# A deformable convolution layer laid out by group and block of rows, with its shift weights built on GpSimd instead of spread by TensorE

## What is computed

```python
G, KS, OM = 8, 3, 32; K = 9; Cg = C // G          # 8 groups of 16 channels, 9 taps
val = xf @ w_value + b_value
om = (xf @ w_off + b_off).reshape(N, P, G, OM)
offset = om[..., :2 * K].reshape(N, P, G, K, 2); mask = om[..., 2 * K:3 * K]
sy = base_y + offset[..., 1]; sx = base_x + offset[..., 0]   # pixel + tap + offset
y0, x0 = floor(sy), floor(sx); ty, tx = sy - y0, sx - x0
for dy, dx, wgt in ((0,0,(1-ty)*(1-tx)), (0,1,(1-ty)*tx), (1,0,ty*(1-tx)), (1,1,ty*tx)):
    acc = acc + gather(y0 + dy, x0 + dx) * (wgt * valid)[..., None]
out = (acc * mask[..., None]).sum(axis=3).reshape(N, P, C) @ w_out + b_out
out = out * inv + (bn_beta - bn_mean * inv)
return out * sigmoid(out)
```

## Time and profile before

| | us |
|---|---|
| runs of the kernel before | 7273.37, 7284.04, 7289.94 |
| the profiled execution's own time | 7276.4 |
| its span (first to last instruction) | 7274.6 |
| TensorE busy, share of span | 5761.8, 79% |
| VectorE busy | 5787.2, 80% |
| ScalarE busy | 5315.5, 73% |
| GpSimd busy | 1442.7, 20% |
| stage of the deformable layer, in the span | 0 to 1160.7 |
| granted clock of TensorE, mean of the span | 0.918 |

### The profile page before, as it was taken

How to read it: one execution, slowest core, us unless ns; L and a number is a source line. 1 busy time by engine, 2 the same in 40 slices (tenths; PEclk the granted TensorE clock), 3 DMA queues, 4 the chain that set the end, 5 groups by cost and what they waited for, 6 DMA issues and landing times. The chain is left out here.

```text
span 7274.6 us, 89393 instructions
## 1 busy us (share of the span) xinstructions
PE 5761.8 (79%) x32962; PEld 2035.3 (28%) x32962; DVE 5787.2 (80%) x12358; ACT 5315.5 (73%) x3820; POOL 1442.7 (20%) x1695
## 2 busy tenths in 40 slices
PE   7888886788769998977777777887777787778787
PEld 3222222344324443422111222222222222222223
DVE  7888887676557765888777788989889898889996
ACT  3332322465545543589999999999999999999996
POOL 3444451000136654610000000000000000000002
PEclk8888887888879998989999999999999999999998
DMA  3111100101000000000000000000000000000000
GB/s 123 50 50 41 53 19 11 30 23 25 12 9 1 1 1 4 1 7 1 1 1 1 1 1 1 1 1 1 12 1 1 1 1 12 1 1 1 1 1 24
DMA packets 45167, 95.26 MB, mean 13 GB/s; under 512 B 7863, under 2 KB 9657, under 8 KB 43578
## 3 DMA queue, kind: packets, MB, share of 16 engines
q1 hardware_dynamic: 43834, 88.44, 3.7%
q0 software_dynamic: 896, 1.06, 0.1%
HBM read 39.14 MB, written 33.55 MB: 10 GB/s over the span
## 5 line engine op out<-in xcount | busy, mean ns | idle before, releaser
L2815 ACT ACTIVATE aa_tanh<-aa_tanh 128x4096 f32<-128x4096 f32 (+5 forms) x1120 | 3671.6, 3368 | 23.6 <-DVE aa_tanh L2995 23.3
L2995 DVE TENSOR_SCALAR aa_tanh<-aa_f_times,aa_g_bias 128x1024 f32<-128x1024 f32 (+18 forms) x5120 | 2986.3, 646 | 475.0 <-PE aa_scores L2861 468.4
L2861 PE MATMUL aa_scores<-aa_tanh,aa_w_spread 128*32 128x512 f32 (+8 forms) x18432 | 2168.4, 584 | 805.7 <-ACT aa_tanh L2815 801.3
L2861 PEld LDWEIGHTS aa_scores<-aa_tanh,aa_w_spread 128*32 128x32 f32 x18432 | 581.0, 112 | 2233.3 <-ACT aa_tanh L2815 1119.8
L2875 PE MATMUL aa_out_sum<-aa_weights,aa_normed 128*128 128x512 f32 (+3 forms) x1152 | 642.8, 642 | 59.6 <-DVE aa_weights L3004 56.9
L2783 POOL TENSOR_SCALAR aa_group_normed<-x_rows,norm_scale,aa_shift_plus 128x128 f32<-128x128 f32 x96 | 92.5, 975 | 2412.4 <-PE aa_turned L2902 1767.3
L860 PE MATMUL near_weights_spread<-near_tap_weights,near_spread_consts 36*64 36x512 f32 x3200 | 429.5, 648 | 66.1 <-DVE near_weighted L507 53.3
L2086 PE MATMUL qa_out<-qa_hidden_rows,qa_weights_in 128*128 128x512 f32 x1024 | 475.3, 607 | 0.0
L880 PE MATMUL near_out_sum<-near_weighted,near_w_out 128*128 128x512 f32 x576 | 359.1, 756 | 103.5 <-DVE near_weighted L507 103.5
L496 DVE TENSOR_TENSOR near_weights_spread<-near_weights_spread,near_values 128x1024 f32<-128x1024 f32 x256 | 314.0, 1227 | 124.1 <-PE near_weights_spread L860 123.6
L427 POOL TENSOR_TENSOR near_tap_weights<-near_hat_y_mask,near_hat_x 128x1024 f32<-128x1024 f32 x144 | 340.0, 2372 | 279.0 <-PE near_weights_spread L860 220.1
(11 more groups left out here) (433 smaller groups left out, 6772.3 us busy)
## 6 DMA issues: line engine op xcount, KB each, us to landing
near_offsets<-near_offset_staged SPq DMA_DIRECT2D x45, 512.0 KB, 3.0
l_taps<-l_scan_in_out SPq DMA_DIRECT2D x256, 64.0 KB, 2.0
x_rows<-in_x SPq DMA_DIRECT2D x4, 2048.0 KB, 15.1
near_offset_y<-near_offsets SPq DMA_DIRECT2D x15, 512.0 KB, 4.0
near_offset_x<-near_offsets SPq DMA_DIRECT2D x15, 512.0 KB, 4.5
near_mask<-near_offsets SPq DMA_DIRECT2D x15, 512.0 KB, 5.4
out_x<-x_rows SPq DMA_DIRECT2D x3, 2048.0 KB, 6.3
out_x<-x_rows SPq DMA_DIRECT2D x8, 256.0 KB, 2.0
```

Source lines behind the costliest of these rows:

```text
L2815: a.activation(TH[:, u % PLACES, 0:length], TH[:, u % PLACES, 0:length], ACT.Tanh).then_inc(th_ready, 1)
L2861: last = t.matmul(sp_[32 * q:32 * q + 32, n % 2, s:e], W2S[:, tt, :], TH[:, p, o + s:o + e], start=tt == 0, stop=tt == 3, tile_position=(0 ...
L2995: ins = v.tensor_scalar(TH[:, p, at[q]:at[q] + w - s], FR[:, m % 2, lo + s:CHUNK], GB[:, key:key + 1], None, ALU.add)
```

## The change

The layout of the work changes. A partition is now (group, block of 4 rows): 8 groups x 16 blocks. A unit is row u of each block, and the free dimension of a product is 16 channels x 64 pixels. Weights of a shift then have 64 elements a partition, and VectorE reads them for each of the 16 channels with step zero. So:

- GpSimd builds the 25 weights of a unit itself: 9 products of hats (128x576, nine taps x 64 pixels), and 9 sums that add each to a 3 x 3 window of the 5 x 5 weights. The spreading matmuls, their constants and the rotating PSUM buffers go.
- Values go to DRAM (`values_at`) and are read back by SP into the new layout, row by row of the blocks, in a ring of 10 rows; offsets and masks are read back 9 rows x 16 blocks at a time, 8 DMAs for each kind. The runs are 64 elements.
- `product` reads both operands from SBUF and writes `PR` or a PSUM buffer `tmp`; `add` comes one shift later. Groups have 2, 1, 2, 1, ... shifts: 16 groups, 9 sums a unit, four buffers `PR`.
- TensorE adds the groups with the identity (`group_out`); ScalarE copies the sum (`keep_sums`, item "e"), SP writes it to DRAM (`sums_at`) and reads it back with channels on partitions (`read_sums`); `out_rows` (item "y") then multiplies by `w_out` and adds the correction for far taps.
- One PSUM buffer `wp` serves all prepared items. `FM` now lies in the buffer of the output `YB`, so that `keep_offsets` waits for `add_out`.
- Batches 1 to 3 of `x` are loaded by ScalarE's DMA queue. The steps for far taps come at other shifts.

The core of the diff:

```diff
-        SIZES = [3] * 7 + [2, 2]
+        SIZES = [2, 1] * 7 + [2, 2]
+            if U and t == 2:
+                items.append(("e", U - 1))
+            if U and t == 12:
+                items.append(("y", U - 1))
+            v = (22, 24) if U == 0 else (6, 8)
+            if u < 2 and b + 1 < NB and t in v:
+                items.append(("v", b + 1, 2 * u + v.index(t)))
+            if t in (16, 18, 20) and U + 4 < NU:
+                items.append(("o", U + 4, KINDS[(t - 16) // 2]))
...
+                        sp.dma_start(O[D_BLK * g:D_BLK * (g + 1), kind, :, :], parked[b][kind, 64 * h + K * gg:64 * h + K * (gg + 1), u, :].rearrange("k (y w) -> y k w", w=WW)).then_inc((ox_loaded, oy_loaded, mk_loaded)[kind], 16)
...
+                    for g in range(G):
+                        rows = values_at[b][D_CG * g:D_CG * (g + 1), j * WW:(j + D_BLK * D_BR) * WW].rearrange("c (y r w) -> y c r w", y=D_BLK, w=WW)[:, :, 0, :]
+                        sp.dma_start(V[D_BLK * g:D_BLK * (g + 1), :, ring_row(b, j) * D_ROWW + D_SPAN:(ring_row(b, j) + 1) * D_ROWW], rows).then_inc(v_loaded, 16)
...
+            def build_step(U, a, b):
...
+                pool.wait_ge(hym, 1 + U * D_NA + a + 1)
+                pool.wait_ge(hx_ready, 1 + U * D_NA + b + 1)
...
+                pool.tensor_tensor(q, HY[:, a, :, :], HX[:, b, :, :], ALU.mult).then_inc(tapped, 1)
+                pool.wait_ge(tapped, 1 + n + 1)
...
+                w = W[:, U % 2, a:a + 3, b:b + 3, :]
+                pool.tensor_tensor(w, w, q.rearrange("p (i j) w -> p i j w", i=3), ALU.add).then_inc(w_ready, 1)
...
+            for U in range(-1, NU):
+                nxt = U + 1
+                if nxt < NU:
+                    clear_weights(nxt)
+                for a in range(D_NA):
+                    if nxt < NU:
+                        mask_hat(nxt, a)
+                    for b in range(D_NA):
+                        if nxt < NU:
+                            build_step(nxt, a, b)
+                        if U > 0 and U % 4 == 0 and (a, b) == (1, 1):
+                            gather_offsets(U // 4)
+                        if U > 0 and U % 4 == 0 and (a, b) == (2, 0):
+                            gather_corners(U // 4)
+                        if U > 0 and (a, b) == (2, 0):
+                            add_out(U - 1)
+                if U == 0:
+                    gather_offsets(0)
+                    gather_corners(0)
...
+                if t == 0:
+                    v.wait_ge(w_ready, 1 + 10 * (U + 1))
...
+                v.tensor_tensor(out.rearrange("p (c w) -> p c w", w=WW), W[:, U % 2, dy + D_SPAN, dx + D_SPAN, :].unsqueeze(1).to_broadcast([P, D_CG, WW]),
+                                V[:, :, at:at + WW], ALU.mult).then_inc(prod, 1)
...
+            CHAIN = {(0, 10): rank_far, (0, 13): select_far, (0, 17): locate, (0, 21): corners, (0, 24): gather_sum, (1, 5): event_values}
+            CHAIN_AGAIN = {(-1, 23): rank_far, (0, 2): select_far, (0, 8): locate, (0, 12): corners, (0, 17): gather_sum, (0, 24): event_values}
...
+                    if t == 22 and U + 4 < NU:
+                        find_far(U + 4)
...
+                if kind == 1:
+                    if U:
                         a.wait_ge(ev_done, 1 + U)
+                    if U >= 5:
+                        a.wait_ge(x_done, 1 + U - 4)
...
+            def hats(U):
+                a.wait_ge(oy_loaded, 1 + 8 * 16 * (U + 1))
+                a.wait_ge(ox_loaded, 1 + 8 * 16 * (U + 1))
+                if U:
+                    a.wait_ge(w_ready, 1 + 10 * U)
...
+                    if t == (10 if U == 0 else 3) and U + 1 < NU:
+                        hats(U + 1)
...
+            def out_rows(U):
...
+                t.wait_ge(sums_in, 1 + 16 * G * (U + 1))
...
+                for s in range(2):
+                    t.matmul(wp[:, s, :], WO[:, :], OUT[:, s * BANK:(s + 1) * BANK], start=True, stop=False)
+                    last = t.matmul(wp[:, s, :], CORR[:, b % 2, :], OH[:, s, :], start=False, stop=True)
...
+                    last = t.matmul(acc[:, s, :], C["ident"], PR[:, gi % NSUM, s * BANK:(s + 1) * BANK], start=g == 0, stop=g == NGR - 1)
```

More of the change, by code:

```diff
@@ L287, in deform_near @@
-        order = list(prep)
+            if U and t == 2:
[7 more added lines that the diff above has]
+                items.append(("o", U + 4, KINDS[(t - 16) // 2]))
+            if U == 0 and t in (12, 15):
+                items.append(("c", 0, (12, 15).index(t)))
@@ L288, in deform_near @@
+            if U == 1 and t in (1, 3, 7):
+                items.append(("c", 0, 2 + (1, 3, 7).index(t)))
+            if b and u == 0 and t in (1, 6, 20, 22):
+                items.append(("c", b, (1, 6, 20, 22).index(t)))
+            if b and u == 1 and t == 3:
+                items.append(("c", b, 4))
+            return items
+        prep = [("b", 0), ("o", 0, 1), ("o", 0, 0), ("o", 0, 2)] + [("v", 0, i) for i in range(4)]
+        first_prep = list(prep)
         for U in range(NU):
             for t in range(NSH):
-                order += [("s", U, t)] + prepared(U, t)
@@ L291, in deform_near @@
                 prep += prepared(U, t)
-        PAIR = {z: i for i, z in enumerate(order)}
-        USE = {z: i for i, z in enumerate(prep)}
-        def spills_done(eng, U, kind):
-            if U == 0:
-                eng.wait_ge(spilled_first, 1 + 3 * 16)
-            else:
-                k = staged(U, kind)
-                eng.wait_ge(spilled[k % 2], 1 + 16 * (k // 2 + 1))
+        for U, kind in ((NU - 1, "e"), (NU - 1, "y")):
+            prep.append((kind, U))
+        in_ring = [z for z in prep if z[0] != "e"]
@@ new lines, in _ @@
+            for z in first_prep:
+                if z[0] in "ov":
+                    spill_item(z)
+                if z == ("o", 0, 2):
+                    for kind in KINDS:
+                        load_offsets(0, kind)
+            sp.wait_ge(padded, 1 + 2 * NB * 16)
+            load_values(0, 0, 8)
+            for U in range(NU):
+                b, u = divmod(U, 4)
+                here = [z for t in range(NSH) for z in prepared(U, t)]
+                if b and u == 0:
+                    load_values(b, 5, 8)
+                if u == 3 and b + 1 < NB:
+                    load_values(b + 1, 4, 5)
+                for z in here:
+                    if z[0] == "e" or (z[0] == "o" and z[1] < 4):
+                        spill_item(z)
+                    if z[0] == "e":
+                        read_sums(z[1])
+                    if z == ("o", 1, 2):
+                        for kind in KINDS:
+                            load_offsets(1, kind)
+                if U:
+                    for z in here:
+                        if z[0] == "v":
+                            spill_item(z)
+                if U + 2 < NU:
+                    load_offsets(U + 2, 1)
+                    load_offsets(U + 2, 0)
+                if u == 2 and b + 1 < NB:
+                    load_values(b + 1, 0, 4)
+                for z in here:
+                    if z[0] == "o" and z[1] >= 4:
+                        spill_item(z)
+                if U == 0:
+                    for z in here:
+                        if z[0] == "v":
+                            spill_item(z)
+                if U + 2 < NU:
+                    load_offsets(U + 2, 2)
```

696 lines of the change are left out of this document (308 added, 388 removed).

## The result

| | before | after |
|---|---|---|
| median of the runs, us | 7278.74 (4 runs, 7273.37 to 7289.94) | 7370.89 (4 runs, 7366.43 to 7373.73) |
| ratio, 95% interval | | 1.0124 (1.0106 to 1.0142) |
| span of the profiled execution, us | 7274.6 | 7368.8 |
| end of the deformable layer in the span | 1160.7 | 1249.7 |
| behind the layer | 6113.9 | 6119.1 |

What follows compares the result with a forecast made beforehand. VectorE bounds the kernel before, TensorE close behind; afterwards VectorE waits for GpSimd. Start 210, units 1 to 14 991, unit 15 40, end 26: 1267 against 1160.7, +106 us, so 7390, range 7265 to 7500.

Steps and rivals of the forecast that it cites:

- The exclusion: VectorE products with both operands in SBUF wait for the running GpSimd instruction; each product getting between costs GpSimd 0.98 us.
- seen in few places: Point in favour of the no-lock rival (products and GpSimd don't exclude each other): -121 us, 7163; chance 0.10.
- GpSimd's 576 columns: GpSimd's instructions of 128x576, which build the weights, take 1.41 us each.
- The path over the addition: Ordinary unit: GpSimd's addition ends at 53.8, then copies, next offsets and far-offset search; 69.1 us against 62.0.
- Far-tap units: First units of later batches carry the far-tap work: 80 us for units 4 and 8, 76 for 12.
- Units 13 and 14: Units with no offsets to make last until GpSimd has the next weights ready, 61.5 us.
- Ranking in units 3, 7 and 11: Ranking adds 3.2 us to each of these units.
- Start: Values go to DRAM and back, SP issuing at 0.6 us each: first product at 106, unit 1 at 210 against 163.
- End: After the last product, sum, spill, read-back, matmuls and output take 26 us, against 6 in the kernel before.
- third rival: 256 B packets take as long as 2 KB ones, first values 100 us instead of 38: 7450 to 7480; chance 0.10.
- a fifth: Small-packet reads stay hidden if a packet costs under a fifth of the 98 ns of 2 KB packets.
- TensorE: A group's pair of matmuls takes 2.7 us; 88 records a unit take 39 to 77 us, some 50 assumed.

Runs made afterwards that it cites:

- Runs 1: Kernel before, with VectorE's product multiplying the values with themselves, both operands in SBUF, instead of with the weights in PSUM: 7472.66 us against 7274.21.
- run 3: Changed kernel, with VectorE copying five shifts' weights at a time to a PSUM bank and products reading them there: 7157.58 us, 0.9841 of before.
- Run 2: Changed kernel, with offset sizes in the buffer of the read-back sums, so the next offsets' copy no longer waits for GpSimd's addition: 7315.95 us.
- run 4: Changed kernel with both edits, offset sizes in the buffer of the read-back sums and weights copied to PSUM: 7118.55 us, 0.9786 of before.

## Why the prediction was right, and where its steps were off

The forecast was 7390 with a layer ending at 1267; measured were 7370.9 and 1249.7. The mechanism was the one predicted, and the terms below are off by amounts that partly cancel. Of the 19 us between the two medians, 5 come from the median of the kernel before, which was taken as 7284.04 and is 7278.74 with a fourth run.

- **The exclusion**. Predicted: VectorE waits for the running GpSimd instruction, which then costs GpSimd 0.98 us. Measured: the product 2.41 instead of 1.22; GpSimd's product of hats 2.38 - 1.40 = 0.98 and its sum 2.26 - 1.40 = 0.86. GpSimd's instructions end 2.34 us apart in the meetings of unit 3 and 1.41 apart on the mean without, whichever they are. So the 0.98 and the 0.86 differ only in when an instruction starts; a product right behind a masking loses 0.86 as well (2.26). Runs 1 and 3 show the cause, one by making it, one by removing it. The prediction rests on one meeting. The trace of before had eleven more at the same search, with a GpSimd masking that began second (some 2.4 us otherwise), on VectorE and GpSimd:

```profile
192.80 1.22 DVE L515 TENSOR_TENSOR near_offset_size<-near_offset_size,near_event_at 128x1024 f32<-128x1024 f32 x1
...
193.54 2.70 POOL L379 TENSOR_TENSOR near_hat_y_mask<-near_hat_y_mask,near_mask 128x1024 f32<-128x1024 f32 x1 [16.33 <-ACT near_hat_y_mask L699]
```

They would have given more weight to the exclusion than "seen in few places". The Trainium skill, "SBUF — State Buffer", Who interferes with whom, has the one that comes second wait until the first is through. VectorE's products lose 1.2 us in a meeting, which agrees. GpSimd loses 0.86 to 0.98 to a product of 1.22, less than the rule gives, and the products at 351.51 and 352.65 ran ahead of a masking that had begun at 350.39, against its order.
- **GpSimd's 576 columns.** 1.41 predicted, 1.40 measured.
- **The path over the addition.** Predicted from a unit's start: addition done at 53.8, the search at 61, unit 69.1. In the unit that starts at 340.3: 52.9, 61.0 and 68.9. Run 2 shows that it was last, and that 61.5 stood next. The unit is right, with small luck inside: GpSimd's first masking came at 10.1 instead of 11.7, its work up to the addition took 0.7 us more than counted, and the way from the addition to the search 1 us more.
- **Far-tap units.** 80, 80 and 76 predicted; GpSimd's clearings give 81.7, 80.4 and 76.7. Units 13 and 14, 61.5 predicted, were 62.0 and 61.3. One part was off: the gathers took 1.70 and 1.49 us on the mean, not the 1.01 and 0.95 of the earlier trace rows.
- **Ranking in units 3, 7 and 11.** Mis-sized: 3.2 us were added for each, but `rank_far` is five instructions of 128x12 or less, over within 0.7 us (407.28 to 408.00 in unit 3), and those units took 68.9 to 69.2. That is most of the difference in units 1 to 14, which took 981.5 us (203.7 to 1185.1), not 991: 9.5 of the 17 us.
- **Start.** First product 106 predicted, 104.06 measured; unit 1 at 210, measured 203.7. SP's issue was taken at 0.6 us and took 33.14 / 64 = 0.52, so the 64 issues end at 99.1 instead of 103, and the offsets of unit 1 are spilled behind them. The start gives 6.3 of the 17 us, mostly so. The timelines of VectorE and SP:

```profile
104.06 1.23 DVE L542 TENSOR_TENSOR near_weighted<-near_shift_weights,near_values 128x1024 f32<-128x1024 f32 x1 [38.87 <-DMA near_values<-near_values]
...
65.96 33.14 SPq L331 DMA_DIRECT2D near_values<-near_values  x64
```

- **End.** 26 predicted, 22.4 measured (last sum over at 1227.3, end 1249.7); the prediction has the last sum, 1.2 us, in both unit 15 and the end. Unit 15 took 42 instead of 40. TensorE's wait for the sums that are read back, inside the end, is 10.3 us.
- **Small packets.** The third rival didn't come. The queue's row on the page:

```profile
q1 hardware_dynamic: 196360, 114.30, 6.6%
```

6.6% x 16 x 7368.8 / 196360 = 40 ns a packet of 582 B on the mean, against 98 ns for 2 KB. Of all packets, 173493 of 198107 are under 512 B (7863 of 45167 before). The rate falls from 21 to 15 bytes a ns, the price of a packet doesn't stay the same. The Trainium skill, "DMA: Bandwidth & Descriptors", Specifications, sets full rate from 512 B; that the rate falls agrees. It stayed hidden: the first product came 5.0 us after the last of the 64 issues. But the margin at the start is thin, and the prediction's "a fifth" was no measure of it (40 is two fifths of 98; 38 us of issues against 100 us of packets make 0.38): from 66 to 99 us the DMA share was 1.30, more than the 16 engines' whole time, so that the times of packets overlap there.
- **TensorE.** 2.7 us for a group's pair predicted; 0.667 x 4 = 2.67 measured, at a clock of 0.83. The range beside it was misread: 88 records are 22 x 1.98 = 44 us at the least, not 39, and 3.51 / 1.98 is 1.77, not the ratio 2 of the clock levels.
- **Behind the layer**, nothing was predicted; 5 us came from there, which no run explains. The runs of the kernel before alone lie 17 us apart.

What the forecast had too much of thus lies in three small terms, the start with SP's issues (6.3), the ranking (7.5 of the 9.5 in units 1 to 14) and the end (3.6), with 2 us back in unit 15; the length of a unit, on which it rested, held.

## What to carry to other kernels

Before moving an operand of a VectorE product from PSUM to SBUF, count the GpSimd instructions that run beside it: each meeting here cost VectorE the rest of the other's run and GpSimd most of the product's, and several products in a row can keep GpSimd out together. If the operand is small and read many times, a copy to a PSUM bank (here 0.48 us for five products) buys the overlap back. And where a buffer is shared by two uses, follow who frees it: an addition off the path became the last wait of every ordinary unit that still had offsets to make.

## What was not expected of the hardware

- GpSimd's gathers suffer from the exclusion too: 1.49 and 1.70 us on the mean beside products with two SBUF operands, 0.99 and 0.99 in run 3, with nothing else changed for them. Whether it is the reading of their row numbers or the making of the transfers that waits, no run separates.
- TensorE's granted clock was higher where the same matmuls stood closer together: over 300 to 900 us it was 0.83 of full speed in the changed kernel (busy 383 us), 0.91 in run 3 (453 us) and 0.94 in run 4 (467 us). Busy time alone doesn't set it: the kernel before, with other matmuls, was busy for 505 us there and had 0.86.
- Three back-to-back products of VectorE, two of them begun later, held up a GpSimd masking for 3.35 us in eight units of the changed kernel and in three of run 2; the reason is open.
